# Turning q and k in squares of 32 through DRAM instead of on TensorE, in a fused attention and gate layer

## What is computed

```python
xn = layernorm(x)                                     # x: 2 x 512 tokens x 512
q = rmsnorm(heads(xn @ Wq.T)) * q_norm_w              # 32 heads of 128
k = rmsnorm(heads(xn @ Wk.T)) * k_norm_w              # 8 heads, one for each 4 of q
v = heads(xn @ Wv.T)
scores = q @ k.T / sqrt(128) + slope[head] * (key - query)      # -1e30 where key > query
s = softmax(scores) @ v, heads side by side, @ Wo.T
low = xn @ A.T                                        # 8 experts of rank 16
g = silu(2 * low, weighted by 8 * softmax(xn @ Wr.T + br), @ B)
y = x + s * g
```

## Time and profile before

| what | value |
|---|---|
| median of 3 runs | 790.67 us (789.51 to 790.70) |
| the profiled execution, its own time | 791.87 us |
| its span, first to last instruction | 789.7 us |
| mean granted clock of PE in it | 0.994 of 2.4 GHz |
| DMA, read and written | 108.67 MB, 138 GB/s on the mean |

### The profile page before, as it was taken

How to read it: one execution, slowest core, us unless ns; L and a number is a source line. 1 busy time by engine, 2 the same in 40 slices (tenths; PEclk the granted TensorE clock), 3 DMA queues, 4 the chain that set the end, 5 groups by cost and what they waited for, 6 DMA issues and landing times.

```text
span 789.7 us, 14690 instructions
## 1 busy us (share of the span) xinstructions
PE 759.3 (96%) x4029; PEld 641.3 (81%) x4029; DVE 512.3 (65%) x1303; ACT 565.0 (72%) x1370; POOL 402.4 (51%) x373
## 2 busy tenths in 40 slices
PE   8888999999999999999999999999999999999987
PEld 7776888888888888888888888888878888888765
DVE  7856666575756757575676758566675856667445
ACT  3657777686777778687776868777775967767853
POOL 4223563464654465455634645554653556445383
PEclk9999999999999999999999999999999999999999
DMA  8015547255453636437362554545364464626511
GB/s 285 2 27 134 173 125 213 79 137 177 137 160 93 195 110 173 119 106 213 98 207 66 163 169 122 157 113 179 106 197 112 107 197 113 201 66 183 154 68 66
DMA packets 148436, 108.67 MB, mean 138 GB/s; under 512 B 44096, under 2 KB 139200, under 8 KB 148288
## 3 DMA queue, kind: packets, MB, share of 16 engines
q1 hardware_dynamic: 148416, 108.43, 47.2%
HBM read 66.18 MB, written 42.21 MB: 137 GB/s over the span
## 4 chain that ended last, share of the span: by engine, by line
PE 51%; issue 23%; POOL 16%; DVE 4%; ACT 4%; DMA 1%; POOLq 0%; SPq 0%; DVEq 0%; ACTq 0%
PE qkv_ps L1070 6%; PE qkv_ps L1071 6%; PE qkv_ps L1072 6%; POOL pt_lo L471 6%; POOL w_lo L449 5%; POOL inv_rms L461 4%; PE out_ps L1070 4%; PE out_ps L1072 4%; PE out_ps L1071 4%; PE score_ps L1070 3%; PE score_ps L1072 3%; PE mix_ps L1070 3%; PE score_ps L1071 3%; PE mix_ps L1072 2%; PE mix_ps L1071 2%
## 5 line engine op out<-in xcount | busy, mean ns | idle before, releaser
L471 POOL TENSOR_TENSOR pt_lo<-x_sb,pt_hi 128x512 fp32r<-128x512 f32 x153 | 193.7, 1293 | 249.8 <-ACT pt_hi L627 249.8
L839 DVE CUSTOM_DVE_ANT_0 probs<-score_ps,cst,slope 128x128 f32<-128x128 f32 (+3 forms) x256 | 131.0, 547 | 137.5 <-PE score_ps L1072 104.9
L1070 PE MATMUL qkv_ps<-w_hi,xt_hi 128*128 128x512 f32 (+1 forms) x512 | 180.3, 352 | 6.3 <-POOL w_lo L449 4.0
L584 ACT ACTIVATE probs<-probs,neg_max 128x128 f32<-128x128 f32 (+3 forms) x256 | 142.0, 556 | 57.9 <-DVE neg_max L839 57.8
L1071 PE MATMUL qkv_ps<-w_lo,xt_hi 128*128 128x512 f32 (+1 forms) x512 | 174.8, 341 | 0.0
L1072 PE MATMUL qkv_ps<-w_hi,xt_lo 128*128 128x512 f32 (+1 forms) x512 | 173.1, 338 | 0.0
L592 ACT ACTIVATE probs<-probs,recip 128x128 f32<-128x128 f32 (+3 forms) x252 | 124.2, 549 | 24.7 <-DVE recip L846 24.7
L1070 PEld LDWEIGHTS qkv_ps<-w_hi,xt_hi 128*128 128x128 f32 x512 | 97.6, 191 | 20.2 <-POOL w_lo L449 5.4
L858 DVE STREAM_TRANSPOSE squared<-probs 128x256 f32<-128x256 f32 (+3 forms) x124 | 100.0, 828 | 17.1 <-ACT probs L592 15.9
L1071 PEld LDWEIGHTS qkv_ps<-w_lo,xt_hi 128*128 128x128 f32 x512 | 97.8, 191 | 10.8
L1072 PEld LDWEIGHTS qkv_ps<-w_hi,xt_lo 128*128 128x128 f32 x512 | 97.1, 190 | 11.4
(11 more groups left out here) (151 smaller groups left out, 1440.7 us busy)
## 6 DMA issues: line engine op xcount, KB each, us to landing
turning<-squared SPq DMA_DIRECT2D x120, 128.0 KB, 2.2
x_sb<-turning SPq DMA_DIRECT2D x30, 512.0 KB, 5.1
w_raw<-wqkv SPq DMA_DIRECT2D x32, 384.0 KB, 4.8
turning<-squared SPq DMA_DIRECT2D x120, 96.0 KB, 1.9
x_sb<-turning SPq DMA_DIRECT2D x30, 384.0 KB, 3.8
turning<-squared SPq DMA_DIRECT2D x128, 64.0 KB, 1.7
x_sb<-turning SPq DMA_DIRECT2D x32, 256.0 KB, 3.0
wo_raw<-wo SPq DMA_DIRECT2D x14, 512.0 KB, 5.9
```

Of the source, the lines that this page charges most:

```text
L471: nc.gpsimd.tensor_tensor(by_quad(pt_lo, j), moved_block(t, j), by_quad(pt_hi, j).bitcast(F32), ALU.subtract).then_inc(pt_lo_by_pool, 1)
L584: nc.scalar.activation(probs[:, h, 0:n], probs[:, h, 0:n], ACT.Exp, bias=neg_max[:, h:h + 1], scale=-1.0, accum_out=total[:, h:h + 1]).the ...
L839: nc.vector.tensor_tensor_reduce(probs[:, h, 0:n], score_bank(t, h), cst[:, C_DIST + SEQ - n:C_DIST + SEQ], slope[:, h:h + 1], HUGE, ALU.a ...
L1070: pe.matmul(out, a_hi, b_hi, start=start, stop=False)
```

## The change

From unit 4 of the run on (`BY_TURN`), q and k are no longer transposed by PE. DVE turns `qk_norm` in squares of 32 into the buffer of the squares (`square_both`), SP writes it to DRAM in four DMAs of 80 KB and reads it back in one of 320 KB into `qk_moved`, and ACT and the low parts read from there. The low part of q is then made by POOL (`moved_q_lo`), that of k still by DVE. Both norm weights are multiplied into k (`both_w`). Since the way is longer, projection and everything up to the square transpose come one unit earlier: slot t projects t+3 and normalizes t+2. The low parts of `wqkv` are made by DVE for chunks 0 and 1 and by POOL for 2 and 3, all in slot t % 8 = 5. The eps is added by POOL instead of standing in a column of the squares. On ACT, `turned_qk_hi(t+1)` now stands ahead of the normalizing of t. In `end`, the order is rewritten around the missing transposes.

The core of the diff:

```diff
@@ sync: one function moves both
+                if u is not None:
+                    sp.wait_ge(qk_squared_ready, ONE(g, u - BY_TURN, 1))
+                    for q in range(QUADS):
+                        sp.dma_start(turning_qk[u % 2, q, :, :].rearrange("(k r) n -> r k n", k=QUADS),
+                                     qk_squared[q * QUAD:(q + 1) * QUAD, :, :]).then_inc(qk_written, 16)
                 for pair in range(2):
                     sp.wait_ge(probs_squared, TWO(g, t, pair + 1))
                     for q in range(QUADS):
+                        if pair == 1 and q == 1 and u is not None and (u - 1) % QB > 0 and u > BY_TURN:
+
+                            sp.wait_ge(q_lo_ready, Q_LO(g, u - 1, 1))
                         sp.dma_start(turning[t % 2, q, :, pair * n:(pair + 1) * n].rearrange("(k r) n -> r k n", k=QUADS),
                                      squared[q * QUAD:(q + 1) * QUAD, :, pair, 0:n]).then_inc(probs_written[pair], 16)
+                if u is not None:
+                    sp.wait_ge(qk_written, QK_WRITTEN(g, u - BY_TURN, 16 * QUADS))
+                    sp.dma_start(qk_moved[:, :, :], turning_qk[u % 2, :, :, :].rearrange("q p n -> p q n")).then_inc(qk_moved_ready, 16)
                 for pair in range(2):
                     sp.wait_ge(probs_written[pair], WRITTEN(g, t, 16 * QUADS))
...
+                if left > 1 and t in (3, 4):
+                    next_w(g, range(2 * (t - 3), 2 * (t - 3) + 2))
+                if here(t, left):
+                    move(g, t, t + 2 if here(t + 2, left) else None)
@@ gpsimd
             def inverse_rms(g, u):
 
                 pool.wait_ge(sums_ready, ONE(g, u, 1))
-                nc.gpsimd.tensor_tensor(inv_rms[:, :], sums[:, :], minus_half[:, 0:NORMED],
+                nc.gpsimd.tensor_tensor(sums_eps[:, :], sums[:, :], eps_sum[:, :], ALU.add).then_inc(eps_added, 1)
+                pool.wait_ge(eps_added, ONE(g, u, 1))
+                nc.gpsimd.tensor_tensor(inv_rms[:, :], sums_eps[:, :], minus_half[:, 0:NORMED],
...
+            def moved_q_lo(g, u):
+
+                if u % QB > 0:
+                    pool.wait_ge(qk_hi_ready, TWO(g, u, 1))
+                    by_quad_of_head = "p (h a n) -> p h a n"
+                    nc.gpsimd.tensor_tensor(q_lo[:, :].rearrange(by_quad_of_head, h=HPG, a=QUADS), turned_qk(u)[0],
+                                            q_hi[:, :].bitcast(F32).rearrange(by_quad_of_head, h=HPG, a=QUADS),
+                                            ALU.subtract).then_inc(q_lo_ready, 1)
...
             def slot(g, t, left):
-                w_due = t % BLOCKS in (5, 6) and here(t - t % BLOCKS + BLOCKS, left)
-                if here(t + 1, left):
-                    inverse_rms(g, t + 1)
-                if w_due and t % BLOCKS == 6:
+                if here(t + 2, left):
+                    inverse_rms(g, t + 2)
+                if t % BLOCKS == 5 and here(t + 3, left):
                     split_w(g + 1, range(EARLY_W, KC))
                 if t % BLOCKS == 2 and here(t, left) and t > 2:
                     split_wo(g + t // BLOCKS, range(0, HPG))
+                if here(t + 1, left) and t + 1 >= BY_TURN:
+                    moved_q_lo(g, t + 1)
                 if here(t - 1, left):
                     turned_lo(g, t - 1)
-                if w_due and t % BLOCKS == 5:
-                    split_w(g + 1, range(0, EARLY_W))
@@ scalar, slot
+                if here(t + 2, left):
+                    square_qk(g, t + 2)
+                    value_hi(g, t + 2)
+                if here(t, left):
+                    exponentials(g, t, range(0, HPG))
+                if w_due:
+                    split_w(g + 1, range(2, 3))
                 if here(t + 1, left):
+                    turned_qk_hi(g, t + 1)
...
@@ vector
+            def square_both(g, u):
+
+                dve.wait_ge(qk_norm_ready, ONE(g, u, 1))
+                nc.vector.transpose(qk_squared.rearrange("p k (h n) -> p h k n", h=NORMED),
+                                    qk_norm[:, :, :].rearrange("p h (k n) -> p h k n", k=QUADS)).then_inc(qk_squared_ready, 1)
+
+            def split_w(group, chunks):
+                for c in chunks:
+                    dve.wait_ge(w_hi_done, group * KC + (c + 1))
+                    nc.vector.tensor_tensor(w_lo[:, c, :], w_raw[:, c, :], w_hi[:, c, :].bitcast(F32),
+                                            ALU.subtract).then_inc(w_lo_by_dve, 1)
...
@@ vector, slot
                 if here(t, left):
                     reciprocals(g, t, 2)
+                if here(t + 2, left):
+                    square_both(g, t + 2)
+                if t % BLOCKS == 5 and here(t + 3, left):
+                    split_w(g + 1, range(0, EARLY_W))
                 if here(t - 3, left):
                     add_out(g, t - 3)
                 if here(t, left):
                     square_probs(g, t, 0)
+                if here(t + 1, left):
+                    turned_qk_lo(g, t + 1)
+                if here(t, left):
                     square_probs(g, t, 2)
@@ tensor, slot
-                if here(t + 1, left):
-                    turn_q(g, t + 1)
-                    turn_k(g, t + 1, left)
-                if here(t + 2, left):
-                    project(g, t + 2)
+                if here(t + 3, left):
+                    project(g, t + 3)
```

More of the change, by code:

```diff
@@ L67 @@
 SILU_SLOT = 4
+BY_TURN = QB
 EARLY_W = 2
@@ L319, in turn_bank, with turned_ps, turned_qk @@
             return (qkv_ps[:, 0, :], qkv_ps[:, 1, :], turn_ps[:, :], score_ps[:, 2, :])[n]
[L321 to L325, removed]
+        def turned_ps(u):
+            return (turn_ps[:, :].rearrange("p (h a n) -> p h a n", h=HPG, a=QUADS),
+                    (score_ps[:, 2, 0:P] if u < 3 else out_ps[:, 0:P]).rearrange("p (a n) -> p a n", a=QUADS))
+        def turned_qk(u):
+            return turned_ps(u) if u < BY_TURN else (qk_moved_by_head[:, 0:HPG, :, :], qk_moved_by_head[:, HPG, :, :])
         def score_bank(t, h):
@@ L419, in _ @@
             sp.wait_ge(xt_turned, BLOCKS)
-            for t in range(3):
-                move_probs(0, t)
+            for t in range(2):
+                move(0, t, None)
+            slot(0, 2, GROUPS)
             pipeline(sp, slot)
@@ L512, in _ @@
             inverse_std(0)
-            split_w(0, range(1))
+            split_first_w(0)
             inverse_std(1)
@@ L664, in slot @@
                     moved_hi(g, t - 1)
-                if w_due and t % BLOCKS == 5:
+                if t % BLOCKS == 4 and here(t + 4, left):
                     split_w(g + 1, range(0, EARLY_W))
@@ L671, in end @@
                 before, last = BLOCKS - 2, BLOCKS - 1
-                square_qk(g, last)
-                value_hi(g, last)
-                exponentials(g, before, range(0, 2))
-                moved_hi(g, before - 1)
+                exponentials(g, before, range(0, HPG))
                 for pair in range(2):
@@ L951, in end @@
                 before, last = BLOCKS - 2, BLOCKS - 1
-                bias(g, before, 0)
-                bias(g, before, 1)
-                square_sums(g, last)
-                value_lo(g, last)
+                for h in range(HPG):
+                    bias(g, before, h)
                 reciprocals(g, before, 0)
-                bias(g, before, 2)
-                bias(g, before, 3)
-                normalize_qk(g, last)
                 reciprocals(g, before, 2)
@@ L962, in end @@
                 mixed_lo(g, before - 2, 1)
-                turned_qk_lo(g, last, 1)
+                turned_qk_lo(g, last)
                 add_out(g, before - 2)
-                bias(g, last, 0, at_end=True)
-                bias(g, last, 1, at_end=True)
+                for h in range(3):
+                    bias(g, last, h, at_end=True)
                 mixed_lo(g, before - 1, 1)
+                bias(g, last, 3, at_end=True)
                 reciprocals(g, last, 0)
-                turned_lo(before, 0)
-                bias(g, last, 2, at_end=True)
-                bias(g, last, 3, at_end=True)
-                for n in range(1, keys_of(before)):
+                for n in range(keys_of(before)):
                     turned_lo(before, n)
@@ L1186, in turn_q, with turn_k @@
                 tr.then_inc(qk_turned, 1)
-            def turn_k(g, u, left=GROUPS):
-                if left == 1 and u == BLOCKS - 1:
-                    pe.wait_ge(v_lo_ready, ONE(g, u, 1))
-                elif u > 3:
-                    pe.wait_ge(acc_ready, 1 + ONE(g, u - 4, 1))
-                pe.transpose(k_turn_ps(u, left), qk_norm[:, HPG, :], ident).then_inc(qk_turned, 1)
+            def turn_k(g, u):
+                if u == 3:
+                    pe.wait_ge(gate_in_kept, BLOCKS)
+                out = (score_ps[:, 2, 0:P] if u < 3 else out_ps[:, 0:P])
+                pe.transpose(out, qk_norm[:, HPG, :], ident).then_inc(qk_turned, 1)
             def turn_probs(t, n):
@@ L1250, in slot @@
```

(22 more changed lines are left out.)

179 lines of the change are left out of this document (110 added, 69 removed).

## The result

The changed kernel takes **827.09 us** (median of 4 runs, 823.55 to 829.22) against 790.41 for the kernel before: ratio 1.0462, 95% interval 1.0418 to 1.0506. The profiled execution is 829.22 with a span of 827.4; before it was 791.87 with 789.7.

A forecast was written before the change was run, and what follows sets the result against it. PE, busy 96% of the span, was taken to bound the kernel. 791.87 - 32.4 (transposes) + 28.0 (q_lo) + 7.5 (clock) + 4.6 (wqkv) + 1.4 (other slots) = 801.0, by the median 800 us; range 778 to 818.

The forecast's parts named there:

- the stall for wqkv: Slot 5, PE waiting for VectorE's first w_lo chunk: 1.2 us against 0.57 that goes, seven times, +4.6 us.
- the price of the clock: PE's granted clock halves after idles over 2 us, 1.5 us each, behind 5 of 7 q_lo stalls: +7.5 us.
- Transposes: On PE, q and k transposes removed from 60 units at 0.54 us each: -32.4 us.
- q_lo behind wo_lo: GpSimd's queue where wo is split: q_lo waits behind four wo_lo, stalling PE 4.0 us seven times, +28.0 us.
- a short stall (A): Rival at wo's split: stall stays 3.4 us, no clock falls, nothing else added; 782 us, chance 0.20.
- no stall (B): Rival: GpSimd's queue order isn't as read, PE never waits, whole gain kept; 760 us, chance 0.05.
- the late bound: In slot 5, VectorE's first w_lo chunk comes at latest 8.8 us in, a stall of 1.5 us at most.
- the +1.4 for other slots: Projection elsewhere waiting for normalize, later still if the probabilities' read is late: 0 to 0.7 us, taken 7 x 0.2.
- after each idle of over 2 us: Rule from two idles of PE in the trace: the granted clock then falls to about half, costing 1.5 us.
- The end: One projection less covers the last softmax; 2 us set against 2 us gained at the start, 4 us of range.
- DMA (C): Rival: DMA becomes the bound, probabilities land late and mix waits in 15 slots; 815 to 830 us, chance 0.12.
- Its own signs: In PE's waits: seven for q_lo, groups some 1 us longer; wrong if over 15 us idle elsewhere.

The follow-up runs named there:

- the mended kernels: Changed kernel with q_lo ahead of wo's split, w_lo ahead of normalize, VectorE's program shorter ahead of the loop, gates a slot earlier: 788.63 us; variants 801.81 and 784.28.
- the kernel with both orders: Changed kernel with GpSimd making q_lo ahead of wo's split and VectorE making its two w_lo right behind v_lo, ahead of normalize: 797.41 us, ratio 1.007.
- the last kernel: Kernel with both orders, shorter VectorE program ahead of the loop and gates a slot earlier, plus the five-scale-factor copy moved from VectorE to ScalarE: 784.28 us.

## Why the prediction was wrong

It said slower, by a mechanism that the runs bear out, and 800 us where 827 came; its range ended at 818. Two terms failed: the stall for wqkv and the price of the clock. The own times differ by 829.2 - 801.0 = 28.2 us.

- **Transposes.** Taken as -32.4; made twice in the kernel before, they add 29.2. Right in kind, 3 us too much.
- **q_lo behind wo_lo.** Forecast seven stalls, 3.4 to 4.3 us with 4.0 taken, 28.0 in all; measured 3.66 to 4.75, 30.2 in all. wo_lo started 7.95 us into the slot and not at 7.14, ScalarE's 1.19 us wait for the moved q among the causes. The read of 320 KB landed after 3.3 us in the median, where 3.4 was taken, so the 2.8 us that the prediction also worked out is too short here. The rivals of a short stall (A) and of no stall (B) fell with these rows.
- **wqkv, the first mis-sized term.** Forecast stalls of 1.2 us with a bound of 1.5, net +4.6; measured 18.3 us in seven, net +14.3. PE was ready at 7.43 us into the slot, as forecast (7.34). The step that failed is the late bound: 7.0 for normalize, plus 0.8, plus 0.9 made 8.8, and w_lo's first chunk was there at 9.6. Normalize ended at 7.0. Between it and the transpose stood set_factor's copy, left out as one of 0.16 us that had been there before, and it took 1.08 beside GpSimd's w_lo. So it is in five of the seven slots, with normalize done at 6.5 to 7.1 and stalls of 1.8 to 2.4 us. In the two longest, 4.2 and 3.3 us, normalize itself was done only at 9.1 and 8.1, past the bound of 7.0: ScalarE had waited 2.5 and 2.7 us for the turned probabilities (`x_sb<-turning`, 20.0 us in the whole run and 2.3 before) and made the squares late. The prediction had a late read of probabilities only in its last term, the +1.4 for other slots. The clock fell behind three of the seven, those of 4.2, 3.3 and 2.1 us, and not behind those of 2.4, 2.3 and 2.2, so its "after each idle of over 2 us" doesn't hold either.
- **The clock, the second.** Forecast 5 x 1.5 = +7.5, for the q_lo stalls alone. The clock fell behind all seven, and behind five of them for about 7 us, which takes 3.4 and not 1.5: 20.5 us in the windows. By the run that kept PE busy they cost 8 to 11 us of time. PE's busy time fell by 12.6 us where -32.4 + 7.5 would have made it 24.9: 12.3 us more are in it. The transposes are little of that, since made twice they raised PE's busy time by 31.7 us (759.3 to 791.0). So about 11.6 of the 12.3 are the clock, 19 us in all. Some 15 of these are behind q_lo: in the run that kept PE busy, its work but for the added matmuls (26.7 us) took 732 us for 746.7. The rest are the falls behind w_lo, behind k_lo and in the start, for which the prediction had no term.
- **The end.** One projection less in front of the last softmax was set against a gain in the start and kept as 4 us of range. PE waited 4.6 us for k_lo at 789 us, and the clock fell there too.
- **Added up:** wqkv 9.7, busy time 12.3, the end 4.6 and q_lo 2.2 make 28.8, for 28.2 to explain.
- **DMA (C)** came out near the 815 to 830 that it named, by another way. The DMA share in a steady stretch rose from 0.50 to 0.67, as forecast, but the mended kernels ran at 0.70 to 0.72 and were 30 us faster. So the DMA engines' share is not the bound. That single reads land late does cost, as in the wqkv slots above.
- **Its own signs.** It would be wrong if PE idled elsewhere for more than 15 us in all, and that came: of 80.7 us of idle 50.5 are not for q_lo, 18.3 of them for w_lo, against 30.4 of idle before. A group got longer by 3.8 to 6.3 us (turns of 95.3 to 97.8 for 91.5) and not by 1.

What the prediction could not have read from its rows is the late start of VectorE in each turn of the loop. It doesn't explain the 827, since the stall for q_lo covered it. In the kernel with both orders its waits are 18.9 us, of which only 5 came back in time when it was taken away; forced on the kernel before, it costs 15 us.

## What to carry over

- Price a moved operation by where it stands in its new engine's queue, and then each stall twice: its length, and the clock behind it. Several terms of a microsecond, each late by a microsecond, were as large here as the one stall that decided.
- When a stall is taken away and less comes back than it lasted, look for "issue" at the first instruction of a loop's turn and at the instruction queue's packets. Code ahead of a loop can be as dear as code in it.
- A copy of VectorE from SBUF to SBUF, or an operation with two inputs in SBUF, has no fixed price while GpSimd runs. Put small ones on ScalarE (0.19 us for the copy there) or where GpSimd is idle.

## What the runs showed of the hardware

**Instruction fetch.** With VectorE's loop at instructions 165 to 443 or 153 to 443 (441 in the last kernel) the instruction queue moves 11 or 12 packets in the whole run; at 171 to 461, 183 to 461 or 171 to 469 it moves 42 to 44 of about 8 KB, and VectorE starts each of six turns late, 2.6 to 3.2 us where it was looked at. A loop of 290 instructions runs without it and one of 278 with it, so the loop's length doesn't decide. Where between 443 and 461 the edge lies wasn't tried. Nor was it tried whether it is the loop's place or the length of VectorE's whole program, which is at most 574 instructions in the runs with 11 or 12 packets and at least 592 in the others. The Trainium skill (Runtime: NRT & Kernel Launch, Instruction fetch mechanics) says that a taken branch whose target has left the window of fetched pages stalls until the page is fetched. The rows agree in kind; its window of two pages of 256 instructions doesn't tell these loops apart, as all of them lie in the first 512.

**VectorE beside GpSimd.** The copy of five columns took 0.16 us in the kernel before, 1.1 in the changed one and 1.8 where GpSimd ran two w_lo back to back; k_lo, with both operands in SBUF, has a median of 0.31 us and once took 1.19, in a mended kernel up to 1.87. The Trainium skill (SBUF — State Buffer, SBUF: two separate sides) says that VectorE's operations in a 2-port mode, or with two inputs in SBUF against a GpSimd operation that reads SBUF, and those of GpSimd take a common pair of ports for a whole instruction, the later one standing still. The times agree: the copy ends with GpSimd's instruction. Not every operation of VectorE within SBUF is slowed: the 60 square transposes of q and k took 0.82 to 0.85 us each in the changed kernel.
